# Rotary rotation of queries and keys moved from GpSimd to ScalarE and VectorE, with the second layer-norm scaling some steps later

## What is computed

```python
q = (x @ wq).reshape(B, T, 16, 128); k = (x @ wk).reshape(B, T, 4, 128); v = (x @ wv)...
cos, sin = _rope_cos_sin(T, D)
q = q * cos + _rotate_half(q) * sin        # _rotate_half(x) = concat(-x[..., 64:], x[..., :64])
k = k * cos + _rotate_half(k) * sin
scores = einsum('bhqd,bhkd->bhqk', q, k) * scale
p_g = softmax(where(causal, scores, neg)); p_l = softmax(where(local, scores, neg))
out = 0.5 * (p_g @ v + p_l @ v)            # local: a causal band over the 256-wide block and 128 before
x1 = layernorm(x + out @ wo)
x_ln = layernorm(x1); logits = x_n @ mu_n; dispatch/combine = softmax(logits over experts / slots)
y = layernorm(x1 + combine @ (W2 gelu(W1 (dispatch^T x_ln) + b1) + b2))
```

## Time and profile before

| | |
|---|---|
| median of 3 runs | 3894.75 us (3891.13 to 4275.52) |
| the profiled execution | 3887.84 us |
| its span, slowest core (7) | 3886.3 us |
| spans of the 8 cores | 3848.1 to 3886.3 us |
| granted TensorE clock of the cores | 0.950 to 0.957 |
| engines busy, share of the span | PE 89%, DVE 36%, ACT 32%, POOL 23% |

### The profile page before, as it was taken

How to read it: one execution, slowest core, us unless ns; L and a number is a source line. 1 busy time by engine, 2 the same in 40 slices (tenths; PEclk the granted TensorE clock), 3 DMA queues, 4 the chain that set the end, 5 groups by cost and what they waited for, 6 DMA issues and landing times.

```text
span 3886.3 us, 66653 instructions; the slowest of 8 cores (3848.1 to 3886.3 us)
## 1 busy us (share of the span) xinstructions
PE 3445.3 (89%) x24864; PEld 2109.2 (54%) x24864; DVE 1382.3 (36%) x3043; ACT 1244.7 (32%) x1700; POOL 898.9 (23%) x993
## 2 busy tenths in 40 slices
PE   7867788988996888878978899999999999999998
PEld 4334545656554445446555555677744455777543
DVE  1334444444433444434545532111135322111244
ACT  1222444446532234434545422212111222221111
POOL 3662344342342443433432200000000000000000
PEclk9888899999998888989999999999999999999999
DMA  9795667474337685685544320367795300677743
GB/s 177 187 210 129 155 171 133 131 166 104 115 114 159 161 182 158 173 121 131 147 107 122 142 104 34 129 239 249 248 324 209 118 33 33 239 249 258 275 154 137
DMA packets 142747, 624.66 MB, mean 161 GB/s; under 512 B 18400, under 2 KB 22496, under 8 KB 119904
## 3 DMA queue, kind: packets, MB, share of 16 engines
q1 hardware_dynamic: 117696, 438.99, 33.6%
q0 software_dynamic: 15520, 114.30, 19.2%
q10 hardware_dynamic: 9216, 67.11, 4.3%
HBM read 612.99 MB, written 188.75 MB: 206 GB/s over the span
## 4 chain that ended last, share of the span: by engine, by line
PE 70%; DMA 11%; DVE 6%; POOL 5%; issue 4%; ACT 3%; DVEq 0%; SPq 0%; ACTq 0%; POOLq 0%
PE ob L1169 12%; PE sc L1079 11%; PE pr L489 9%; PE pr L400 9%; PE sc L1373 6%; PE sc L591 4%; PE ob L619 4%; DMA x1sp<-AR 4%; PE pr L1373 3%; PE ob L1373 3%; PE sc L1220 3%; DMA AR<-wqkv_c 3%; DMA AR<-xT_r 2%; PE pr L432 2%; POOL AR L377 2%
## 5 line engine op out<-in xcount | busy, mean ns | idle before, releaser
L595 ACT ACTIVATE AR<-sc 128x1024 bf16<-128x1024 f32 (+2 forms) x640 | 564.0, 895 | 509.2 <-PE sc L591 498.8
L400 PE MATMUL pr<-AR 128*128 128x512 bf16 x2560 | 655.4, 398 | 61.8 <-DMA AR<-xT_r 19.4
L489 PE MATMUL pr<-AR 128*128 128x512 bf16 x2048 | 530.9, 397 | 50.2 <-DMA AR<-wo 25.2
L1169 PE MATMUL ob<-AR 128*128 128x256 bf16 x4096 | 459.6, 273 | 0.0
L619 PE MATMUL ob<-AR 128*128 128x129 bf16 x3840 | 309.4, 227 | 163.3 <-DVE AR L665 106.3
L1079 PE MATMUL sc<-AR 128*128 128x512 bf16 x2048 | 452.5, 379 | 0.0
L479 POOL TENSOR_TENSOR AR<-AR 128x2 f32<-128x2 f32 x64 | 45.0, 703 | 1680.4 <-DVE AR L475 1639.4
L1169 PEld LDWEIGHTS ob<-AR 128*128 128x128 bf16 x4096 | 399.4, 98 | 54.6
L400 PEld LDWEIGHTS pr<-AR 128*128 128x128 bf16 x2560 | 247.1, 102 | 314.2 <-issue 115.0
L591 PE MATMUL sc<-AR 128*128 128x256 bf16 (+1 forms) x2304 | 357.5, 279 | 55.5 <-ACT AR L595 44.7
L619 PEld LDWEIGHTS ob<-AR 128*128 128x128 bf16 x3840 | 258.5, 101 | 250.9 <-issue 196.7
(11 more groups left out here) (96 smaller groups left out, 3796.7 us busy)
## 6 DMA issues: line engine op xcount, KB each, us to landing
AR<-w_c SPq DMA_DIRECT2D x256, 512.0 KB, 6.2
AR<-wqkv_c SPq DMA_DIRECT2D x160, 512.0 KB, 5.4
w_c<-W_r POOLq DMA_DIRECT2D x32, 2048.0 KB, 19.8
AR<-x SPq DMA_DIRECT2D x32, 1024.0 KB, 6.1
x1sp<-AR ACTq DMA_DIRECT2D x32, 1024.0 KB, 6.5
AR<-b SPq DMA_DIRECT2D x32, 1024.0 KB, 10.3
AR<-x1sp SPq DMA_DIRECT2D x32, 1024.0 KB, 4.9
out<-AR ACTq DMA_DIRECT2D x32, 1024.0 KB, 3.9
```

The costliest lines, as they stand in the source:

```text
L400: tm = p.pe(lambda e, b=b, c=c, w=w, xt=xt: e.matmul(out=pr[b], lhsT=w[:, c * 128:(c + 1) * 128], rhs=xt[:, c * 512:(c + 1) * 512], start= ...
L489: tm = p.pe(lambda e, b=b, h=h, dg=dg, nt=nt, i=i: e.matmul(out=pr[b], lhsT=oT[i % 2][:, nt, h, :], rhs=wo[h][:, dg * 512:(dg + 1) * 512], ...
L595: ta = p.act(lambda e, b=b, eb=eb, lo=lo, hi=hi: e.activation(out=eb[:, lo:hi], in_=sc[b][:, 0:hi - lo], func=AF.Exp), tm, t_E_pe[h % 2])
L1169: tm = p.pe(lambda e, b=b, s=s, c=c, n=n, gp=gp: e.matmul(out=ob[b][:, s * 256:(s + 1) * 256], lhsT=rx[n][:, c * 128:(c + 1) * 128], rhs=E ...
```

## The change

The rotation leaves POOL. ACT now makes three copies out of PSUM per projection: the f32 one as before, and the two halves, each written 64 partitions away as bf16 into `t2v`. The bank is given back after the third. DVE multiplies `qraw` by cos, `t2v` by sin in place, and adds: three operations, the products two ticks after the copies and not one, the sum three ticks after and not six. The host's table of sin has its sign on the other half, since the multiplication now follows the move. The count `ropes` makes the load of the next cos and sin wait until all products are written out. The later steps of the first-stage layer norm move: second scaling from ticks 20 and 23 to 26 and 28, statistics, store and reload to 31, 34 and 40; as it now lasts longer, the two tiles have a scale buffer `rs` each. In window 2 six key and value projections come before the first output projection. `scale_all` in window 14 starts 8 ticks later.

```diff
-    sin[64:] *= -1.0
+    sin[:64] *= -1.0
...
-        rs = v(CONST + 1232, F32, 2)
+        rs2 = [v(CONST + o, F32, 2) for o in (1232, 832)]
...
+            while ropes[0]:
+                tick()
             p.dma("sync", "D_cs", cosv, d_cs[0][:, g * 512:(g + 1) * 512], t_rope[0])
...
-            ta = p.act(lambda e, b=b, i=i: e.activation(out=qraw[i], in_=pr[b], func=AF.Copy),
-                       tm, t_qraw[i])
+            p.act(lambda e, b=b, i=i: e.activation(out=qraw[i], in_=pr[b], func=AF.Copy),
+                  tm, t_qraw[i])
+            for o in (0, 64):
+                ta = p.act(lambda e, b=b, i=i, o=o: e.activation(
+                    out=t2v[i][o:o + 64, :], in_=pr[b][64 - o:128 - o, :], func=AF.Copy), t_t2[i])
             give_pr(b, ta)
             tok = {}
+            ropes[0] += 1
 
             def products():
+                ropes[0] -= 1
                 tok[1] = p.dve(lambda e: e.tensor_tensor(out=dst, in0=qraw[i], in1=co,
                                                          op=ALU.mult), ta, tcs[0], *toks)
-                p.pool(lambda e: e.tensor_tensor(out=t2v[i][0:64, :], in0=qraw[i][64:128, :],
-                                                 in1=si[64:128, :], op=ALU.mult),
-                       ta, tcs[0], t_t2[i])
-                tok[2] = p.pool(lambda e: e.tensor_tensor(out=t2v[i][64:128, :],
-                                                          in0=qraw[i][0:64, :],
-                                                          in1=si[0:64, :], op=ALU.mult))
-                t_qraw[i] = t_rope[0] = [tok[1], tok[2]]
+                tok[2] = p.dve(lambda e: e.tensor_tensor(out=t2v[i], in0=t2v[i], in1=si,
+                                                         op=ALU.mult), ta, tcs[0])
+                t_qraw[i] = tok[1]
+                t_rope[0] = tok[2]
...
-            after(1, products)
-            after(6, total)
+            after(2, products)
+            after(3, total)
...
-            for n_, fn in ((1, power), (2, bias), (3, apply), (20, lambda: second(0)),
-                           (23, lambda: second(1)), (26, stats), (30, store), (38, reload)):
+            for n_, fn in ((1, power), (2, bias), (3, apply), (26, lambda: second(0)),
+                           (28, lambda: second(1)), (31, stats), (34, store), (40, reload)):
                 after(n_, fn)
...
+                if i == 2:
+                    yield from kv[0:6]
+                    for n in range(8):
+                        yield out[n]
+                        yield from kv[n + 6:n + 7]
+                    return
...
             if i == 14:
-                scale_all()
+                after(8, scale_all)
```

More of the change, by code:

```diff
@@ L302, in build_program @@
         rn_q = [0]
+        ropes = [0]
         q_made = set()
@@ L476, in ln_stats, with ln_pow, ln_bias @@
                                                    scalar2=LN_EPS, op0=ALU.mult, op1=ALU.add), t)
-        def ln_pow(t):
+        def ln_pow(t, rs):
             return p.pool(lambda e: e.tensor_tensor(out=rs, in0=pw, in1=mhalf, op=ALU.pow), t)
-        def ln_bias(t):
+        def ln_bias(t, rs):
             return p.dve(lambda e: e.tensor_scalar(out=nb, in0=mv[:, 0:1], scalar1=rs[:, 0:1],
@@ L509, in ln1 @@
             xl = xlb[nt]
+            rs = rs2[nt]
             tok = {}
@@ L513, in power @@
             def power():
-                tok["p"] = ln_pow(tok["w"])
+                tok["p"] = ln_pow(tok["w"], rs)
             def bias():
-                tok["b"] = ln_bias(tok["p"])
+                tok["b"] = ln_bias(tok["p"], rs)
             def apply():
@@ L1334, in ln2 @@
                 y = y2[row[n]]
+                rs = rs2[n % 2]
                 tok = {}
                 tok["w"] = ln_stats(t6, (st6, st6b)[n % 2])
-                tok["p"] = ln_pow(tok["w"])
+                tok["p"] = ln_pow(tok["w"], rs)
                 t_s6[n % 2] = tok["p"]
                 def fin():
-                    tb = ln_bias(tok["p"])
+                    tb = ln_bias(tok["p"], rs)
                     tx = p.act(lambda e: e.activation(out=y, in_=y, func=AF.Identity, bias=nb,
```

## The result

The changed kernel is 0.64% faster than the one before: the ratio of its time to that of before is 0.9936, with a 95% interval of 0.9917 to 0.9955, which is 25 us (18 to 32). I had forecast 3846 against 3894.75 us, a ratio of 0.9875. So the direction was right, and the size about half of what I gave. (The plain median of its ten runs, 3975.09 us, is no measure of the change: half of them had one die at a lower clock, and such runs of both kernels are left out of every ratio here.)

A forecast was written before the change was run, and what follows sets the result against it. PE was taken as bound by late arrivals in the first stage, not throughput. Terms -18 -20 +24 -14 -10 +4 -4 = -38 us idle, times 1.3 about -49 us: 3846 against 3894.75 us; 8-in-10 range 3785 to 3903 us.

The forecast's parts named there:

- the clock's 1.3: First stage: each microsecond of PE idle time removed gives back 0.3 to 0.4 us more through the clock; factor 1.3.
- The bound: Only the first stage changes: at most its 412 us of PE idle time and the clock's cost there are at stake.
- GpSimd without the rotation: First stage, POOL's rotation gone: PE's waits for masks -18 us and for divisions -20 us.
- The copies: First stage, ACT's two extra copies: late transposes +8 us, late exps +8 us, DVE's later first product +8 us; together +24 us.
- a sign that I had named for being wrong: First stage: the forecast would be wrong if ACT's waits exceeded 90 us.
- Products two ticks after the copies: First stage: DVE's first product waits for three copies, the extra 1.2 us covered only in part by the extra tick: +8 us.
- rival D: Slower: exps wait behind ACT's two more copies, DVE's products behind them; 3939 us at half exposed; chance 0.10, slower half copies included.
- The second scaling later: First-stage layer norm, second scaling six ticks later: DVE's wait for row stores -33 us, PE's idle time -14 us.
- Window 2: Key projections first: the 12.47 us wait for a `pr` bank gone or shortened, -10 us; waiting for slabs +4 us.
- The start: PE's wait for `wo`: POOL issues its load up to 5 us earlier without rotations, but transfers fill the time; -4 us.
- DVE's third operation: First stage, new 16-bit product on DVE: 488 ns each, 78 us of DVE's time, costed at nothing further.
- stay for the most part: First stage: PE's long waits behind row stores remain mostly, since the scaling's 3.3 us delay doesn't cover 20 us.

The follow-up runs named there:

- e7: Kernel before, GpSimd's two rotation products left out of the computation with nothing in their place: ratio 0.9808 to the kernel before, -75 us.
- e3: Changed kernel without the two 64-partition copies on ACT, moved halves left out of the computation: ratio 0.9808 to the kernel before.
- e4: Changed kernel with each 2 MB conversion of expert weights cut in four of 512 KB: ratio 0.9863 to the kernel before.
- e13: e10 without the two 64-partition copies, moved halves left out of the computation: ratio 0.9741 to the kernel before.
- e10: e4 with DVE's products at tick 3 and the sum at tick 4, each one tick later: ratio 0.9825 to the kernel before.
- e9: e4 with both DVE products one tick after ACT's copies and not two: ratio 1.0069 to the kernel before.
- e1: Changed kernel with only the rotation changed, layer norm ticks, window 2 and scale_all put back: ratio 0.9923 to the kernel before.
- e2: Kernel before with only the second scaling moved later and two scale buffers, rotation still on GpSimd: ratio 0.9984 to the kernel before.
- e5: Changed kernel with only the layer norm's ticks put back: no interval; its two comparable executions took 3876.84 and 3881.71 us.
- e12: Changed kernel with window 2's order, scale_all and the reload put back, rotation and later scaling kept: ratio 0.9913 to the kernel before.

## Why the prediction was right, and where not

The sign and the bound were right, the size was half. Two misses cancel almost wholly, the gain without POOL's rotation (18 us too small) and the price of the copies (19 us too small); that is luck. What is missing from the forecast is about what I had credited to the later scaling and to window 2 (18 and 8 us with the clock's 1.3), for which the runs show nothing.

- **The bound.** Right: only the first stage changed. It ends 24.5 us earlier in the mean over the cores, the whole gain; the second stage is as it was.
- **GpSimd without the rotation: -38 us, times 1.3 -49.** Too small. e7 measured 67 us in the stage and 75 in the time. POOL's busy time was as forecast (477.5 us for 470). The two waits that I had priced came near in e7: divisions -15 us for my -20, masks -16 for -18 (in the changed kernel masks fell only from 24.6 to 13.4 us). What the sum had at nothing is the rest of the fall of 46 us in PE's waits, the scores' wait for a rotation's sum the clearest part of it. And a microsecond of wait gave back more than 1.3 there: 67 us for 46 is 1.46. Elsewhere the same quotient of stage to waits is 1.5 (e3 against the changed kernel), 1.4 (e4 against it) and 1.0 (e13 against e10), so 1.3 is no more than a middle.
- **The copies: +24 us, times 1.3 +31.** The mechanism was right, the size off: 50 us, by e3 and e13. Their duration and sum were right (591 ns, 189.0 us, the free size decides). The step that failed is "only a transpose that takes the bank just left waits": PE waits 34.1 us in the mean for the copies, in transposes and in projections both, and 25 us more for exps. With PE's waits for ACT at 125.7 us and not under 90, a sign that I had named for being wrong appeared.
- **Products two ticks after the copies.** I gave this +8 us, as covered "only in part". e9 shows that it is the step on which the sign of the change hangs: at tick 1 the price is 80 us more. My rival D had its mechanism right (DVE's products behind ACT's list), and with the old tick it comes true, even with the conversions split (e9, 27 us slower than before).
- **The second scaling later: -14 us.** Failed. DVE's wait fell by more than the 33 us I had worked out (75.0 to 27.6 us), but e1 and e2 show no gain to speak of, and e5 and e12 none that they agree on. I had taken PE's wait after a store's stall as the price of the stall. In e2 the next wait, for ACT, takes its place.
- **Window 2: -6 us.** Not shown. The 12.47 us stall of the earlier trace rows didn't go, it moved: on core 6 of the changed kernel DVE waits 10.35 us for a store until 451.29 us, and PE stands still for 14.72 us.
- **The start: -4 us.** Right in kind. The last load of `wo` is issued at 255.82 us and no longer at 265.02, and the output projection starts at 276.56, 7.6 us earlier; PE's wait is 20.1 us.
- **DVE's third operation.** 430 ns, below my 488; the product with cos 692 ns. On core 7 of the kernel before, 149 of the 160 products with cos ran beside an instruction of POOL, at 785 ns, and the other 11 took 684. The rule of the Trainium skill that the doubled rate needs 16-bit operands ("VectorE: DVE Perf Modes", "What auto-detection actually checks") fits 430 ns beside 692. The sum is at 520 ns where it was 488, which is 5 us over the stage. It doesn't meet the masks more often (56 of 160 times in the mean over the cores, 64 before), but a meeting costs more: 705 ns where it was 454. With POOL at rest it takes 423 ns and took 421; gone are 13 meetings with a rotation, at 1110 ns. That a DVE instruction with two inputs in SBUF contends with a GpSimd instruction that reads SBUF is what the Trainium skill says ("SBUF — State Buffer", "Who interferes with whom"), and the 705 against 423 ns agree. Why a meeting got dearer isn't shown.
- **What I didn't weigh** is that the time is that of the slowest of eight cores. A stall of 30 us that strikes one core in some place costs the whole kernel nearly all of it. The long stalls that "stay for the most part", as I wrote, were worth about as much as the largest terms of my sum: e4 took them away and gained 0.7% on the changed kernel, 29.5 us in the stage.

## What to carry to other kernels

Where an engine runs a hand-ordered list, an instruction that waits is priced by what stands behind it: put it a step or two behind its producer, and measure one step on either side, since here one place in the list was worth 2% and DVE's and ACT's busy times told nothing of it (1424.6 and 1439.8 us in e4, 1416.9 and 1441.2 in e9). Moving work off a shared helper onto an engine that feeds the critical one is a trade of two large numbers (70 against 50 us here), so measure each alone by leaving it out. Cut big background transfers into pieces before moving the waits that they cause.

## What was not expected of the hardware

- Conversion DMAs of 2 MB hold up a 1 MB store on another queue: issued between two of them, it landed after 40.9 us, where the median is 6.6 us. With the conversions in pieces of 512 KB, the same bytes in the same windows, the latest landing of such a store was 21.2 us and the longest wait for one 10.4 us (27.3 and 19.0 us in the kernel before with the same edit).
- ACT's copy of 64 partitions, moved by 64, takes 591 ns, as long as one of 128 partitions (596 ns).
- With all cores at clocks of 0.954 to 0.958, the slowest core of an execution can be 56 us behind the fastest (3820.7 and 3876.7 us). A single stall behind a store explains half of that. It isn't the only source: e10 has no wait for a store above 9.2 us, and its cores lie between 3785.5 and 3836.3 us. What sets them apart there isn't shown.
